# A two-layer graph network, linear attention and a quantised feed-forward on one core: the second graph layer's products as seven block products for a pair of row tiles

## The reference

```python
xn = layernorm(x)
deg_inv = 1 / max(in_degree, 1)
def sage(h, W_self, W_neigh, b):
    mean = segment_sum(h[src], dst) * deg_inv
    return h @ W_self + mean @ W_neigh + b
h   = relu(sage(xn, W_self0, W_neigh0, b0))
gnn = sage(h, W_self1, W_neigh1, b1)
mix = attention_without_softmax(xn)          # relu(q), relu(k), (k^T v) first
x   = x + gnn + mix
# feed-forward: weights rounded to -1, 0, 1 times their mean magnitude,
# activations rounded to integers by their row's largest value
x   = x + bitlinear(gelu(bitlinear(layernorm(x), w1)), w2)
```

## Time and profile before

| | |
|---|---|
| time, median of 3 runs | 1321.35 us (1321.3 to 1321.87) |
| span of the profiled execution | 1319.4 us |
| PE busy | 1314.5 us, 6490 matmuls |
| DVE busy | 879.3 us |
| ACT busy | 475.0 us |
| POOL busy | 3.8 us |
| granted TensorE clock | 1.000 |

### The profile page before, as it was taken

The page is one execution under the profiler, slowest core; times in us unless marked ns, Lnnn a source line. Parts: engine busy times, 40 slices in busy tenths (PEclk is TensorE's granted clock), DMA queues, the critical chain, the costliest instruction groups (busy, mean ns, idle before and its releaser), DMA issues.

```text
span 1319.4 us, 19208 instructions
## 1 busy us (share of the span) xinstructions
PE 1314.5 (100%) x6490; PEld 627.2 (48%) x6490; DVE 879.3 (67%) x1526; ACT 475.0 (36%) x709; POOL 3.8 (0%) x16
## 2 busy tenths in 40 slices
PE   9999999999999999999999999999999999999999
PEld 5454445555445444444444444444444444444444
DVE  7854542352677767767879858855877567886774
ACT  7765565355213233321211112210000076464460
POOL 0000000000000000000000000000000000000000
DMA  8487886765044541014766864645545409723523
GB/s 351 147 281 265 272 274 227 296 212 181 24 158 156 181 145 48 17 27 139 207 179 194 227 176 159 223 156 199 179 151 175 131 30 296 144 56 96 128 54 107
DMA packets 173196, 219.93 MB, mean 167 GB/s; under 512 B 93889, under 2 KB 127425, under 8 KB 171841
## 3 DMA queue, kind: packets, MB, share of 16 engines
q1 hardware_dynamic: 132992, 209.00, 48.4%
q10 hardware_dynamic: 40128, 9.97, 4.4%
HBM read 164.41 MB, written 32.51 MB: 149 GB/s over the span
## 4 chain that ended last, share of the span: by engine, by line
PE 99%; DVE 1%; DMA 0%; issue 0%; ACT 0%; DVEq 0%
PE ps L1749 54%; PE ps L2000 13%; PE ps L2088 9%; PE ps L2125 9%; PE ps L1880 8%; PE ps L1947 2%; PE ps L1888 1%; PE ps L1801 1%; PE ps L1783 1%; DMA XIN<-in_x 0%; DVE Zb L1013 0%; PE ps L2170 0%; PE ps L1770 0%; DVE st L977 0%; DVE XH L1008 0%
## 5 line engine op out<-in xcount | busy, mean ns | idle before, releaser
L1749 PE MATMUL ps<-S,XH 128*128 128x512 f16 x2400 | 526.6, 379 | 0.0
L1749 PEld LDWEIGHTS ps<-S,XH 128*128 128x128 f16 (+1 forms) x2400 | 234.3, 98 | 277.3
L2000 PE MATMUL ps<-Zb,AT 128*128 128x512 f16 x800 | 175.4, 379 | 0.0
L2000 PEld LDWEIGHTS ps<-Zb,AT 128*128 (+1 forms) x800 | 78.2, 98 | 94.1
L1749 PE MATMUL ps<-S,Zb 128*128 128x512 f16 x480 | 106.4, 379 | 0.0
L1880 PE MATMUL ps<-XH,S 128*128 128x512 f16 (+1 forms) x576 | 102.6, 339 | 0.0
L1749 PE MATMUL ps<-Zb,XH 128*128 128x512 f16 x432 | 94.8, 379 | 0.0
L1274 DVE TENSOR_SCALAR STREAM<-tables,keys 128x320 f16 x240 | 71.4, 298 | 25.5 <-issue 13.2
L1395 DVE SCALAR_TENSOR_TENSOR STREAM<-STREAM,cols 128x1024 fp8e4<-128x1024 f32 x64 | 79.2, 1278 | 0.0
L1880 PEld LDWEIGHTS ps<-XH,S 128*128 128x128 f16 x576 | 56.1, 98 | 47.0 <-issue 2.3
L1749 PEld LDWEIGHTS ps<-S,Zb 128*128 128x128 f16 x480 | 47.0, 98 | 54.4 <-issue 0.6
(11 more groups left out here) (248 smaller groups left out, 1422.9 us busy)
## 6 DMA issues: line engine op xcount, KB each, us to landing
STREAM<-in_w1t SPq DMA_DIRECT2D x64, 512.0 KB, 5.0
STREAM<-in_w2t SPq DMA_DIRECT2D x52, 512.0 KB, 4.4
STREAM<-in_w_all SPq DMA_DIRECT2D x48, 512.0 KB, 5.3
XIN<-in_x SPq DMA_DIRECT2D x20, 512.0 KB, 5.3
SPLIT<-in_Wneigh SPq DMA_DIRECT2D x16, 512.0 KB, 5.8
SPLIT<-in_Wself SPq DMA_DIRECT2D x16, 512.0 KB, 4.4
w1q_scratch<-STREAM SPq DMA_DIRECT2D x16, 512.0 KB, 5.0
w2q_scratch<-STREAM SPq DMA_DIRECT2D x16, 512.0 KB, 3.7
```

Of the source, the lines that this page charges most:

```text
L1749: last = mm(acc[:, n * BANK:(n + 1) * BANK], left(l, kc), right(kc, r)[:, n * BANK:(n + 1) * BANK], start=(kc == 0 and i == 0), stop=(kc = ...
L2000: last = mm(banks(bank + n, 1), AT_tile(t, s), Z[:, r, s, n * BANK:(n + 1) * BANK], start=(s == 0 and r == 0), stop=(s == NT - 1 and r == 1))
```

## The change

The layer-1 products h W_self1 and h W_neigh1 are made per pair of row tiles by seven products of 128x512 by 512x512 blocks in place of eight (Winograd's form of Strassen's scheme). For that: the weights' blocks and their differences are prepared by DVE and ACT, split in hi and lo, stored to DRAM and loaded as slots (`prep_*`, `block_load`); the pair's row blocks and their sums are made in `h_sums`, split, and transposed by six DMA transposes a pair; ten groups of seven products follow (`st_pe`, five pairs for self, five for neighbours); ACT and DVE combine them (`st_copy`, `c11` to `c21`). The self rows of layer 1 are added to `u_scratch` in DRAM by GpSimd DMAs. Self product and neighbour product of layer 0 change places: `s0_pe` runs between the counts, its rows go to DRAM; `z0_pe` follows, then ten edge sums in a row. The rounding of the feed-forward weights changes: ACT rounds (two activations) and clips from below (two more), DVE clips from above and makes the differences. Quads 0 to 5 stand in the s0 stage, 6 to 9 beside the edge sums, 10 to 31 beside the block products.

Core of the diff (a line `...` stands for what is left out):

```diff
+EARLY_QUADS = 6
+EDGE_QUADS = 10
+        S0_QUADS = {t: t - 3 for t in range(3, 9)}
+        H_QUADS = {t: EARLY_QUADS + t // 2 for t in range(1, NT - 2, 2)}
+        ST_QUADS = ((10, 11), (12, 13), (14, 15), (16, 17), (18, 19), (20, 21), (22, 23, 24), (25, 26), (27, 28, 29), (30, 31))
...
# SP
             def quad_load(i):
+                k = quad_before(i)
+                if k is not None:
+                    sp.wait_ge(S("made"), 4 * k + 1)
...
+                if i == EDGE_QUADS + 1:
+                    sp.wait_ge(S("h_turned1"), 64 * PAIRS)
...
+            sp.wait_ge(S("g0_ps"), NT)
+            for name in LOAD_ORDER[3:]:
+                block_load(0, name)
+            quad_load(EDGE_QUADS + 1)
...
+            def st_quads(i):
+                for n in ST_QUADS[i]:
+                    quad_load(n + 2)
+                    quad_store(n)
...
# ACT
+            def quad_round(i, part):
+                w, n = i // W1_QUADS, part % 2
+                piece = quad_raw(i)[:, n, :]
+                if part < 2:
+                    act.wait_ge(S(f"piece_in{2 * quad_at(i) + n}"), 16 * quad_nth(i) + 32)
+                    A(piece, piece, ACT.Identity, bias=col("magic"), scale=col("isw")[:, w:w + 1]).then_inc(S("rounded"), 1)
+                else:
+                    act.wait_ge(S("rounded"), 4 * i + n + 1)
+                    A(piece, piece, ACT.Relu, bias=col("to_pos")).then_inc(S("rounded"), 1)
...
             for t in range(NT):
-                if t > 0:
-                    z_act("z0", t - 1, 4 * ((t - 1) % 2), Z0_SCALE)
                 if t < KC:
-                    split_chunk(weight(S1), t, t % 2, 32 + t, at("s", WS0))
+                    split_chunk(weight(S1), t, t % 2, 32 + t, at("s", WN0))
                 counts_act(NT + t)
                 if NT + t < 2 * HC - U_FIRST:
                     late_sum(NT + t)
+                if t in S0_QUADS:
+                    for part in range(4):
+                        quad_round(S0_QUADS[t], part)
...
+            def st_copy(i, which):
+                product, to = (("P1", held_1), ("P6", held_2), ("P5", held_3))[which]
+                act.wait_ge(S("st_ps"), st_done(i, product))
...
+                A(to, banks(st_banks(i)[0], 1), ACT.Copy, scale=...).then_inc(S("st_act"), 1)
+            def h_act(p):
+                for j in range(2):
+                    # relu in place, hi part (whole row or second half), square with sum
...
+                    if j == 0:
+                        # two transposes (nc.scalar.dma_start_transpose) after h_lo
...
+                if p == PAIRS - 1:
+                    act.wait_ge(S("c_x"), 1)
+                    st_copy(0, 0)
+                act.wait_ge(S("h_sums"), 4 * p + 4)
+                A(HL[:, 1, 0, 0:BANK], sum_rows[:, 3 * BANK:4 * BANK], ACT.Copy).then_inc(S("h_hi"), 1)
+                A(more_rows[:, 0, :], sum_rows[:, 0:3 * BANK], ACT.Copy).then_inc(S("h_hi"), 1)
+            def h_turn(p):
+                # two transposes of 128x1024, two of 128x1536
...
+            for p in range(PAIRS):
+                h_act(p)
+                for t in (2 * p, 2 * p + 1):
+                    if t in H_QUADS:
+                        for part in range(4):
+                            quad_round(H_QUADS[t], part)
+                h_turn(p)
...
+            def st_act(i):
+                rounds = [later_round(k, part) for k in ST_QUADS[i] for part in range(4)]
...
+                if i > 0:
+                    st_copy(i, 0)
+                some(0, 2)
...
+                some(2, 4)
...
+                some(4, 5)
...
+                some(5, 6)
+                st_copy(i, 1)
+                some(6, 10)
+                st_copy(i, 2)
+                some(10, 12)
...
# DVE
+            dve.wait_ge(S("stream_used"), 8 * NORMS + HC)
+            V.tensor_reduce(col("w1_sum"), MW[:, 0, :], AXX, ALU.add).then_inc(S("w_sum"), 1)
             q_dve(2, 0)
...
             for t in range(NT):
-                counts_dve(NT + t, lambda: z0_dve(t))
+                counts_dve(NT + t, lambda: s0_dve(t))
                 for s in SUMS_AT.get(t, ()):
                     source_sum(s)
+                if t in S0_QUADS:
+                    quad(S0_QUADS[t])
...
+            for p in range(PAIRS):
+                h_rows(2 * p)
+                h_quad(2 * p - 1)
+                h_left(p)
+                h_rows(2 * p + 1)
+                h_sums(p)
...
+            def st_dve(i):
+                quads = list(ST_QUADS[i])
+                c11(i)
+                if i > PAIRS:
+                    z1_lo_rest(i - 1)
+                quad(quads[0])
+                if i >= PAIRS:
+                    z1_lo_first(i)
+                c22(i)
+                for n in quads[1:]:
+                    quad(n)
+                c12(i)
+                c21(i)
...
# PE
             pe.wait_ge(S("kv_sq"), 1)
-            total(5, col("kv_sq"), 1)
+            pe.wait_ge(S("w_sum"), 1)
+            total(5, cols[:, first_col["kv_sq"]:first_col["kv_sq"] + 2], 2)
             q_pe(3, 1)
...
+            for t in range(1, NT):
+                wait(pe, "h_t1", t - 1)
+                edge_sum(t, edge_bank(t), z0_of, "g0_ps")
...
+                for kc in range(KC // 2):
+                    for n, (l, r) in enumerate(((0, 0), (0, 1), (1, 0))):
+                        last = mm(banks(to, 1), left(l, kc), W[:, kc, r, :], ...)
...
+            def st_pe(i):
+                st_product(i, "P2", b)
+                pe.wait_ge(S("st_act"), 3 * i + 1)
+                st_product(i, "P6", a, False, False)
+                st_product(i, "P7", c, stop=False)
+                pe.wait_ge(S("st_act"), 3 * i + 2)
+                st_product(i, "P5", a, False, False)
+                if i + 1 < 2 * PAIRS:
+                    st_first(i + 1)
+                pe.wait_ge(S("st_act"), 3 * i + 3)
+                st_product(i, "P3", a, False)
+                pe.wait_ge(S("st_c"), 4 * i + 2)
+                st_product(i, "P4", c, False)
...
+            for t in range(1, NT - 2):
+                wait(pe, "x1", t - 1)
+                edge_sum(t, x1_bank(t), z1_of, "g1_ps")
...
             for g in range(2):
                 f1_pe(0, g)
-            pe.wait_ge(S("x1_t1"), NT)
-            s1_pe(8)
+            pe.wait_ge(S("x1"), 8)
+            edge_sum(8, x1_bank(8), z1_of, "g1_ps")
             pe.wait_ge(S("f1_d"), 12)
-            s1_pe(9, 0)
+            edge_sum(9, x1_bank(9), z1_of, "g1_ps")
```

More of the change, by code:

```diff
@@ L473, in hid_turn @@
+            for t in range(NT - 2):
+                x1_moves(t)
             def hid_turn(t, half, product):
@@ L1428, in _ @@
[L1428 to L1430 removed]
+            dve.wait_ge(S("stream_used"), N_SUMS)
+            V.tensor_reduce(col("w2_sum"), MW[:, 1, :], AXX, ALU.add).then_inc(S("w_sum"), 1)
+            for t in range(NT):
+                if t < KC:
+                    prep_dve(t)
+                if t == 2:
+                    dve.wait_ge(S("norm_ps"), 6)
+                    w_mean(1, ps[:, MEAN_AT:MEAN_AT + 1])
+                    degrees()
+                z0_lo(t)
@@ new lines, in h_quad, with row_half, rows_free @@
+            def h_quad(t):
+                if t in H_QUADS:
+                    quad(H_QUADS[t])
+            for p in range(PAIRS):
+                h_rows(2 * p)
[3 more added lines that the diff above has]
+                h_sums(p)
+            def row_half(i, row, half):
+                return pair_rows[i % 2][:, row, half * BANK:(half + 1) * BANK]
+            def rows_free(i):
+                wait(dve, f"s1_out{i % 2}", 32 * (i // 2))
+                if i == 1:
+                    dve.wait_ge(S("h_sq"), NT)
+                    dve.wait_ge(S("h_hi"), 4 * PAIRS)
@@ L2032, in _, with edge_sum @@
-            pe.wait_ge(S("z0_lo"), NT)
-            edge_sum(0, "g0_ps", 4)
-            h_pe(1, 1, first=True)
-            steps(pe, 2, NT, h_pe)
-            def z1_pe(t, j, between={}):
-                wait(pe, "z1_lo", t - 1)
-                pe.wait_ge(*hT_in(t, j))
-                product(banks(4 * j), of_x(t), of(weight(S0)), between=between).then_inc(S("z1_ps"), 1)
+            for t in range(1, NT):
+                z0_pe(t)
+            def edge_sum(t, bank, right, name, ready=None):
+                for s in range(NT):
+                    if ready is not None:
+                        ready(s)
+                    for r in range(2):
+                        for n in range(2):
+                            last = mm(banks(bank + n, 1), AT_tile(t, s), right(r, s, n),
+                                      start=(s == 0 and r == 0), stop=(s == NT - 1 and r == 1))
+                last.then_inc(S(name), 1)
```

909 lines of the change are left out of this document (569 added, 340 removed).

## The result

The changed kernel takes **1449.74 us** (median of 4 runs, 1448.56 to 1454.65) against 1321.38 us for the kernel before (1321.3 to 1321.87): ratio 1.098, 95% interval 1.096 to 1.100, so 128 us slower. The forecast was 1407 us, range 1358 to 1440: right in its direction, 43 us short in size and outside its range. The runs also scatter more, by 6 us where the kernel before scatters by 0.6.

A forecast was written before the change was run, and what follows sets the result against it. PE's own instructions were taken to bound the kernel, any PE wait being lost whole. Terms -25.9 + 4.3 + 38.9 + 1.1 + 46.5 + 11.8 + 8.6 = +85.3 gave span 1404.7, time 1406.7 us; range 1358 to 1440.

The forecast's parts named there:

- wait 3: Edge sums and first block group: ACT's list, held by transposes, makes PE wait 46.5 us (39 to about 75).
- wait 5: Start of the feed-forward: P6 waits for tile 7's row, transpose and first copy, no longer covered by edge sums, +8.6 us.
- quad terms: Early quads' delays: quads 0 to 3 6.9 us each, quad 4 6.2, quad 5 4.9, summed as 38.9 us.
- row at the feed-forward: Tile 7's row on DVE, its transpose on ACT and the first copy, taken as 11.2 us, less 2.6 of products.
- Saving: Layer 1's block products: 840 matmuls instead of 960, 120 fewer at 0.216 us each, 25.9 us less.
- Wait 1: In q, PE wants `w_sum` at 273.3 us but DVE's preceding edge-list boundary ends at 277.6, +4.3 us.
- Wait 2: Early quads: late ACT roundings delay DVE's one-hot tables for PE's counts, +38.9 us, plus 1.1 for scale work; lower bound 5.
- Wait 4: Block groups 6 to 9 with three quads: late quad loads delay ACT's copies, +11.8 us (0 to 16).
- The clock rival: Clock falls during PE's long waits, so first products after them run slower: +16 us, 1423 us; chance 0.2.
- GpSimd's additions: Block groups: additions over 9 us would make `c11` wait; in a rival with ACT's transposes, 1425 us, chance 0.12.
- ACT's transposes back up: Edge sums: `h_turn` near 10 us instead of 7.5 gives +15 to +25, 1425 us; chance 0.12, shared with GpSimd's additions.

The follow-up runs named there:

- edit (1): In the changed kernel, the total of the weights' sums in q formed five chunks into the next product; measured only together with two other edits, 1436.8 us.
- run 6: Changed kernel with q's total formed later, both first-group copies before quad 11's roundings, and T1's second load issued before the first half's last quads: 1436.8 us.
- run 1: Changed kernel with ScalarE rounding each early quad before the tile's count copies instead of after them: 1402.5 us.
- run 2: Changed kernel with 26 all-zero matmuls added on PE before the first count part behind each of the six early quads: 1436.3 us.
- run 3: Changed kernel with all 30 transposes of the edge stage issued from SyncE's queue instead of ScalarE's: 1417.2 us.
- run 5: Changed kernel with quad 9's store, quad 10's load and all four block loads waiting until pair 4's first two transposes have landed: 1441.2 us.
- run 7: Changed kernel with edge sum 8 ahead of the first feed-forward groups and edge sum 9 in another bank: 1453.9 us.
- run 10: The combined kernel with block loads and quads reordered after the edge sums, edge sum 8 in its own bank, and ScalarE's first two feed-forward copies earlier: 1369.8 us.
- the combined kernel: Changed kernel with the edits of run 1, run 3, run 6 and run 7, T3 and T1 loaded ahead of the last pair's transposes: 1356.4 us, ratio 1.027.

## Why the prediction was right in its direction and short in size

**The mechanism** was right: everything was hidden behind PE, so every late operand would be lost whole. The waits sum to 125 us against 111 forecast, and 14 + 29 is the 43 us missed. Two steps failed. The matmuls behind the waits stood in the sum at nothing; they cost 29.2 us, and only a rival had them. And the issue of a transpose was a fixed price: for pair 4's first two 2.8 us were taken, and they took 20.6. That is most of the 9.9 us by which wait 3 came out dearer; wait 5 adds 6.2, 3.4 of them through a row that began later than taken and 2.9 at the next pair. Two of the forecast's sums are off by 0.2 us at most (its quad terms give 38.7, its row at the feed-forward 11.05), which changes nothing.

**Saving, -25.9.** Right: block products and both sets of edge sums run at 0.216 us a matmul once PE is warm; the moving operand in four pieces costs nothing:

```profile
1098.64 69.23 PE L2438 MATMUL ps<-XH,AT 128*128 128x512 f16 x320
```

69.23 / 320 = 0.216.

**Wait 1, in q, +4.3.** Right, 5.2; edit (1) of run 6 removes it.

**Wait 2, the early quads, +38.9 and 1.1.** Near in sum, 38.3 against 40.0: six of 5.1 to 6.7 us and one of 0.9, released by VectorE's tables. That is in part luck: the second count part, for which 0.7 us was taken four times, never waited, and the first waited up to 0.5 us longer than the 6.2 taken. The cause named (roundings behind the last count copy) is shown by run 1, and the bound given for it, 5 us left, was 4.5. What was missed is its second price, 13.4 us of slow matmuls (runs 1 and 2).

**Wait 3, ACT in the edge sums, +46.5 (39 to 75).** The place and the engine were right (run 3), the size was not: 6.1 + 34.8 + 15.5 = 56.4 us of waits and 7.4 of slow pieces, 63.8 in all. ScalarE's path, followed, held up to pair 4: the relu of pair 4 began at 860.7, 107.4 us after the first edge sum, where 110 was forecast. The step that failed comes behind it. Pair 4's two narrow transposes took 20.6 us where the earlier trace rows gave 2.8, so the copy for P6 ended at 134.8 instead of near 119. `h_turn` took 7.0 to 7.3 us in the first three pairs, near the 7.5 taken, then 10.2 and 6.1. The forecast treated the issue of a transpose as a fixed price per form; run 5 (2.65 us for the same two) shows that it depends on what else is on the DMA engines, and the four block loads that SyncE issues at that very moment stood in the diff. Row and quad loads lengthen it too: issued by SyncE in run 3, the same form took 2.7 us in pair 0, before the first quad's load, and 6.6 to 7.4 in pairs 1 to 4. SyncE's three in a row, 9.75 us, may have been a hint that a queue stands still; the forecast read it as a matter of shape, and as a rival.

**Wait 4, three quads in a group, +11.8.** Near in sum, 10.9 us of waits, and wrong in its make-up: the three-quad groups cost 1.9 + 1.9 + 0.8 = 4.6, the other 6.3 were T1's second load, issued behind the quads' moves. That load was not costed: of the moved steps SyncE's queue was followed for the quads alone. Run 6 moved it ahead of the quads' moves; then a quad's load came late, and ScalarE's copy with it, 7.1 us.

**Wait 5, start of the feed-forward, +8.6.** 11.9, and 2.9 more at the next pair. VectorE begins tile 7's row at 1172.0, 4.3 us after its edge sum ended at 1167.7; 0.9 was taken. Runs 7 and 10 show more than was forecast: neither of two other orders made up for the cover that was lost, two products.

**The clock rival, +16 at a chance of 0.2.** It was real. It took 1.3 us a wait, half of the full 2.6. Measured by balance it is 29.2 us, 2.7 for each of the eleven waits of over 4 us, so near the full price. (Start to start, the matmuls are some 25 us late against their warm spacing; the rest is the last matmul before each wait, whose 379 ns the busy time counts whole.) The twelve matmuls behind the waits of 6.4, 15.5 and 34.8 us took 4.55, 5.30 and 4.95 us instead of 2.75, and the edge sum behind one of 2.3 us 10.49 instead of 8.81. The rule of the Trainium skill beside it (TensorE: Matmul & The Clock Gate, part 1) spoke for it, and the trace of the changed kernel agrees, and the chance given, with no row in the trace of before that could show a wait, was too low: with twelve long waits forecast, the forecast itself had made the condition of the rule.

**The other rivals.** GpSimd's additions held nothing that PE waited for: they are not among PE's releasers in the block groups. "ACT's transposes back up" (0.12) was right in kind, and looked in the wrong place: it put the time into `h_turn`, and the two that backed up most are those of `h_act` in pair 4.

**Left open.** Whether another placement of the 26 later quads, for instance beside z0, where the DMA share is 0.72 and PE never waits, would bring the kernel below 1321 us was not tried. Open too is why the same two transposes beside the same traffic take from 10.5 to 22.4 us, and what makes the rate of full DMA engines fall to 103 GB/s. No run here beats the kernel before; the nearest full one is the combined kernel, 1356.4 us.

## What to carry to other kernels

A kernel that keeps PE busy for 99.6% of its span has no slack left: take a gain in matmuls only after following every engine's list and every DMA queue through the new order, and book each forecast wait twice, once as idle time and once as the slow matmuls behind it. Ask of each stage what its DMA engines carry, in share and in GB/s: here transposes and loads delayed each other, whichever queue they were on, and a queue that issues a transpose should have nothing urgent behind it. When a product that covered another engine's tail is removed, its cover is part of its price; and when several waits share one cause, moving one load or one copy may only move the wait, as in runs 3, 6 and 7. Read what an edit gave from its own stage: the whole time also holds what changed elsewhere by chance, as in run 2.

## What was not expected of the hardware

The issue of two 128x1024 transposes takes an engine's queue 2.65 us with nothing else under way, and 10.5 to 22.4 us beside four 1 MB block loads and a quad's load and store (20.6 in the changed kernel); ScalarE computes nothing meanwhile. At a DMA share above 1 the DMA engines moved 103 GB/s in one stretch and 410 in another. PE idle from 864 to 885 us is granted 0.50 of its clock, and twelve matmuls behind a wait take up to 5.30 us instead of 2.75. Matmuls with an all-zero stationary operand were enough to keep the granted clock at 1.00.
